# Experts in tiles of 256 rows instead of 384, with three of eight weight chunks split in advance and read back as halves

## What is computed

```python
h = h + attn(layernorm(h))                       # softmax(q k^T + causal) v, 16 heads
# mixture of experts, x = layernorm(h), E=4, K=2, D=256, F=1024
top_p, top_i = top_k(softmax(x @ router_w + router_b), 2);  top_p /= sum(top_p)
out = sum_e gate[t, e] * ((silu(x @ w1[e]) * (x @ w3[e])) @ w2[e])
h = h + out
h = h + recurrence(layernorm(h))
h = h + quantised_ffn(layernorm(h))
```

## Time and profile before

| | |
|---|---|
| median of three runs | 1753.79 us (1750.0 to 1754.49) |
| the profiled execution's own time | 1756.17 us |
| its span | 1754.3 us, 30236 instructions |
| granted TensorE clock, mean | 0.92 of full speed |
| TensorE busy | 1476.7 us, 84% of the span |
| VectorE, ScalarE, GpSimd busy | 1223.8, 989.0, 927.4 us |
| attention | about 86 to 830 us |
| expert stage, first to last matmul | 848.6 to 1394.8 us |
| recurrence and quantised layer | 1404 us to the end |
| DMA in all | 150.38 MB, mean 86 GB/s |

### The profile page before, as it was taken

How to read it: one execution, slowest core, us unless ns; L and a number is a source line. 1 busy time by engine, 2 the same in 40 slices (tenths; PEclk the granted TensorE clock), 3 DMA queues, 4 the chain that set the end, 5 groups by cost and what they waited for, 6 DMA issues and landing times. The chain is left out here.

```text
span 1754.3 us, 30236 instructions
## 1 busy us (share of the span) xinstructions
PE 1476.7 (84%) x10725; PEld 1374.2 (78%) x10725; DVE 1223.8 (70%) x2590; ACT 989.0 (56%) x2138; POOL 927.4 (53%) x750
## 2 busy tenths in 40 slices
PE   5389999999999999995699999999988746789039
PEld 4279888888888888885699999999987745788039
DVE  7548677777777777774256666666588489459896
ACT  4547675757575757572455555555543444459552
POOL 4468475858585858572567677776755623000000
PEclk8679999999999999997799999999999968899569
DMA  7490000000000100001665555555544321003313
GB/s 241 147 309 19 19 19 28 28 28 28 28 28 25 31 25 14 25 13 34 193 167 142 138 146 136 148 135 149 140 122 107 66 89 43 11 0 133 110 51 113
DMA packets 86126, 150.38 MB, mean 86 GB/s; under 512 B 7992, under 2 KB 63608, under 8 KB 85720
## 3 DMA queue, kind: packets, MB, share of 16 engines
q1 hardware_dynamic: 75464, 134.62, 24.7%
q0 software_dynamic: 10512, 13.83, 4.6%
HBM read 111.88 MB, written 49.91 MB: 92 GB/s over the span
## 5 line engine op out<-in xcount | busy, mean ns | idle before, releaser
L1589 POOL TENSOR_TENSOR expert_w_low<-expert_raw,expert_w_high 128x768 fp32r<-128x768 f32 x152 | 288.5, 1948 | 172.1 <-ACT expert_w_high L1414 167.0
L855 ACT ACTIVATE expert_raw<-psum,neg_max 120x376 f32<-120x376 f32 (+2 forms) x384 | 176.9, 486 | 106.0 <-DVE neg_max L1041 103.8
L1561 DVE TENSOR_TENSOR expert_act_low<-expert_act,expert_act_high 128x384 fp32r<-128x384 f32 x152 | 140.0, 921 | 79.6 <-ACT expert_act_high L1452 79.0
L1452 ACT ACTIVATE expert_act_high<-expert_act 128x384 fp32r<-128x384 f32 x152 | 79.8, 525 | 204.1 <-DVE expert_act L1556 202.7
L967 POOL TENSOR_TENSOR qk_low<-rotated,qk_high 128x376 fp32r<-128x376 f32 x128 | 127.0, 992 | 95.2 <-ACT qk_high L848 95.2
L1373 PE MATMUL psum<-slots_high,expert_w_high 128*128 128x384 f32 x608 | 161.0, 346 | 16.7 <-DVE expert_act L1556 15.4
L1064 DVE TENSOR_TENSOR pt_low<-psum,pt_high 128x752 fp32r<-128x752 f32 x128 | 120.4, 941 | 69.9 <-ACT pt_high L864 69.5
L1373 PE MATMUL psum<-slots_low,expert_w_high 128*128 128x384 f32 x608 | 157.0, 339 | 0.0
L1373 PE MATMUL psum<-slots_high,expert_w_low 128*128 128x384 f32 x608 | 156.7, 338 | 0.0
L1384 PE MATMUL psum<-expert_w_high,expert_act_high 128*128 128x256 f32 x456 | 134.5, 295 | 11.6 <-ACT slot_out L1434 9.9
L997 POOL TENSOR_TENSOR rotated<-rotated,expert_raw 128x376 f32<-128x376 f32 x128 | 127.7, 998 | 14.5 <-POOL expert_raw L993 0.5
(11 more groups left out here) (305 smaller groups left out, 4380.6 us busy)
## 6 DMA issues: line engine op xcount, KB each, us to landing
expert_raw<-in_experts SPq DMA_DIRECT2D x152, 384.0 KB, 3.1
x_slots<-in_c_slots SPq DMA_DIRECT2D x4, 3168.0 KB, 27.8
slot_rows<-x_slots SPq DMA_DIRECT2D x19, 396.0 KB, 4.5
up_spill<-held SPq DMA_DIRECT2D x5, 1128.0 KB, 5.0
held<-up_spill SPq DMA_DIRECT2D x5, 1128.0 KB, 5.7
attn_x<-tok_xt SPq DMA_DIRECT2D x6, 752.0 KB, 4.0
x_parts<-attn_x SPq DMA_DIRECT2D x6, 752.0 KB, 4.6
patch<-in_patches SPq DMA_DIRECT2D x8, 376.0 KB, 6.8
```

Source lines behind the costliest of these rows:

```text
L855: last = act.activation(probs[0:ni, h % 2, at:at + P * it + ni], score_bank(h % 2, it), ACT.Exp, bias=neg_max[0:ni, h % 2, it:it + 1], acc ...
L1561: dve.tensor_tensor(act_hl[1][:, g % 2, :], act_f[:, g % 2, :], act_hl[0][:, g % 2, :].bitcast(F32), ALU.subtract).then_inc(low_made, 1)
L1589: pool.tensor_tensor(w[1][:, g % RING, :], raw[:, g % RAW, :], w[0][:, g % RING, :].bitcast(F32), ALU.subtract).then_inc(w_low, 1)
```

## The change

There are two edits that belong together.

**Tiles of 256 rows.** TILE_SLOTS goes from 384 to 256. EXPERT_TILES becomes 27 (before 19), BLOCKS 2 (before 3); rows of all tiles go from 7296 to 6912, chunks from 152 to 216, and weight loads with them. All ACT, DVE and PE work that goes by TILE_SLOTS gets 256 columns; the split of a weight chunk keeps its 768.

**Chunks 2, 4 and 6 are split once** (KEPT_SPLIT). There are 4 experts times 3 such chunks, 12 jobs, two at the beginning of each of batches 1 to 6. A job loads the chunk over `whole` (columns of `expert_raw` that held the raw and swapped projections), ACT copies it into `parts[0]` (`pt_high`), POOL makes `parts[1]` (`pt_low`), and SP stores both to `split_w` in DRAM. The second job of a batch uses the same buffers, and step (b, 0) of ScalarE waits until all of it is stored. In the expert stage these chunks come as two halves, 768 KB, straight into `both` (`expert_w`), after `down` of the chunk eight before; ACT and POOL no longer split them.

Two small tables (`past`, `place`) move into `resid`.

```diff
-TILE_SLOTS = 384
+TILE_SLOTS = 256
...
+KEPT_SPLIT = (2, 4, 6)
+KEPT_RAW = tuple(f for f in range(CHUNKS) if f not in KEPT_SPLIT)
+SPLIT_JOBS = [(e, k) for e in range(EXPERTS) for k in range(len(KEPT_SPLIT))]
+SPLIT_BATCHES = range(1, 1 + len(SPLIT_JOBS) // 2)
...
@@ attention
+        whole = shared[:, 0:CHUNK_COLS]
+        parts = [x[:].rearrange("p u k n -> p (u k n)")[:, 0:CHUNK_COLS] for x in pt]
...
+                def load_whole(j):
+                    e, k = SPLIT_JOBS[j]
+                    sp.dma_start(whole, a["experts"][e, KEPT_SPLIT[k], :, :]).then_inc(whole_in, 16)
+
+                def store_parts(j):
+                    e, k = SPLIT_JOBS[j]
+                    sp.wait_ge(parts_low, j + 1)
+                    for part in range(2):
+                        sp.dma_start(split_w[e, k, :, part, :], parts[part].bitcast(F32)).then_inc(parts_stored, 16)
+
                 for b in range(BATCH + 1):
+                    if b in SPLIT_BATCHES:
+                        sp.wait_ge(rot_made, 16 * b + 2 * LEAD + CR_ROT)
+                        load_whole(2 * b - 2)
+                        store_parts(2 * b - 2)
+                        load_whole(2 * b - 1)
+                        store_parts(2 * b - 1)
                     if b:
                         sp.wait_ge(out_kept, T * b)
...
+                def split_part(j):
+                    act.wait_ge(whole_in, 16 * (j + 1))
+                    act.wait_ge(parts_stored, 32 * j)
+                    act.activation(parts[0], whole, ACT.Copy).then_inc(parts_high, 1)
+
                 def begin(b):
                     for at, t in enumerate(VALUE_ORDER):
+                        if at == 1 and b in SPLIT_BATCHES:
+                            split_part(2 * b - 2)
+                            split_part(2 * b - 1)
...
+                    if c == 0 and b in SPLIT_BATCHES:
+                        act.wait_ge(parts_low, 2 * b)
+                        act.wait_ge(parts_stored, 64 * b)
                     turned_high(b, 2 * c)
...
+                def split_part(j):
+                    pool.wait_ge(parts_high, j + 1)
+                    pool.tensor_tensor(parts[1], whole, parts[0].bitcast(F32), ALU.subtract).then_inc(parts_low, 1)
...
+                        if n == 2 * LEAD - 1 and b in SPLIT_BATCHES:
+                            split_part(2 * b - 2)
+                            split_part(2 * b - 1)
...
@@ expert_tiles
                         g = CHUNKS * i + f
-                        if g >= RAW:
-                            sp.wait_ge(w_low, g - RAW + 1)
...
+                        if f in KEPT_SPLIT:
+                            if i:
+                                sp.wait_ge(down_made, g - RING + 1)
+                            k = KEPT_SPLIT.index(f)
+                            sp.dma_start(both[:, f, :, :].bitcast(F32), split_w[bass.ds(e, 1), k, :, :, :]
+                                         .rearrange("e p h c -> p (e h) c")).then_inc(split_in[k], 16)
...
-                    if g + AHEAD < last_chunk:
+                    if g + AHEAD < last_chunk and (g + AHEAD) % CHUNKS in KEPT_RAW:
                         split_high(act, g + AHEAD)
...
-                    if g + AHEAD < last_chunk:
+                    if g + AHEAD < last_chunk and (g + AHEAD) % CHUNKS in KEPT_RAW:
                         split_low(g + AHEAD)
```

More of the change, by code:

```diff
@@ L432 @@
 RAW_CHUNKS, EARLY_CHUNKS, AHEAD_ROWS = 4, 2, 4
+KEPT_SPLIT = (2, 4, 6)
+KEPT_RAW = tuple(f for f in range(CHUNKS) if f not in KEPT_SPLIT)
+SPLIT_JOBS = [(e, k) for e in range(EXPERTS) for k in range(len(KEPT_SPLIT))]
+SPLIT_BATCHES = range(1, 1 + len(SPLIT_JOBS) // 2)
 SHARED_COLS = 5 * TOK + 2 * (3 * P + TOK)
 def attention(nc, psum, h0_rows, x_dram, weights, a, consts, ident, x_slots, h_rows, onehot, where, shared, raw_w, w_in,
-              scattered, tables, made):
+              split_w, scattered, tables, made):
     ctx, sb, sem = scopes(nc, made)
@@ L484, in attention @@
         ends = sb("tile_ends", [P, EXPERTS])
-        past = sb("past", [P, EXPERT_TILES, EXPERTS])
+        past = resid[:, 0, 0:EXPERT_TILES * EXPERTS].rearrange("p (t e) -> p t e", e=EXPERTS)
         owner = sb("owner", [P, EXPERT_TILES])
         start_of = sb("start_of", [P, EXPERT_TILES])
-        place = sb("place", [P, 2, EXPERT_TILES])
+        place = resid[:, 1, 0:2 * EXPERT_TILES].rearrange("p (k t) -> p k t", k=2)
         slots_cleared = sem("slots_cleared")
+        whole_in, parts_high, parts_low, parts_stored = (sem(f"split_w_{n}") for n in ("in", "high", "low", "stored"))
         (summed, std_made, rstd_made, x_made, x_turned, xt_kept, logits_made, odds_read, shifted, odds_made,
@@ L1254, in _, with expert_tiles @@
                 dve.wait_ge(table_made, 1)
-def expert_tiles(nc, psum, a, x_slots, h_rows, onehot, where, raw, w_in, added, ident, vec, first, turn, feed, up_gate, down,
+def expert_tiles(nc, psum, a, x_slots, h_rows, onehot, where, raw, w_in, split_w, added, ident, vec, first, turn, feed, up_gate, down,
                  spent, made):
@@ L1264, in expert_tiles @@
         xt = [sb(f"slots_{part}", [P, 2, 2, TILE_SLOTS], F32R) for part in ("high", "low")]
-        w = [sb(f"expert_w_{part}", [P, RING, CHUNK_COLS], F32R) for part in ("high", "low")]
+        both = sb("expert_w", [P, RING, 2, CHUNK_COLS], F32R)
+        w = [both[:, :, part, :] for part in range(2)]
         silu = sb("silu", [P, 2, TILE_SLOTS])
@@ L1302, in group_dst @@
             return dst if len(dst.shape) == 3 else dst.rearrange("p (k n) -> p k n", k=GROUP)
+        split_in = [sem(f"expert_split_in{k}") for k in range(len(KEPT_SPLIT))]
+        raw_of = lambda g: len(KEPT_RAW) * (g // CHUNKS) + KEPT_RAW.index(g % CHUNKS)
         three = ((0, 0), (0, 1), (1, 0))
@@ L1435, in keep_out @@
                                    scale=gate[:, i % 2, 1:2]).then_inc(y_kept, 1)
-                split_high(act, 0)
-                split_high(act, 1)
-                keep_high(0, 0)
-                keep_high(0, 1)
-                split_high(act, 2)
-                split_high(act, 3)
+                for g in range(AHEAD):
+                    if g == EARLY_CHUNKS:
+                        keep_high(0, 0)
+                        keep_high(0, 1)
+                    if g in KEPT_RAW:
+                        split_high(act, g)
                 for g in range(last_chunk):
@@ L2311, in audio_tower @@
             attention(nc, psum, h0_rows, x_dram, weights, a, consts, ident, x_slots, h_rows, onehot, where, shared,
[L2312 removed]
+                      raw_w, w_in, split_w, scattered, tables, front_sems)
         held = ctx.enter_context(nc.sbuf_tensor("held", [P, UPS * QCHUNKS * TOK], F32))
@@ L2323, in audio_tower @@
             expert_sems, late_sems = [], []
-            expert_tiles(nc, psum, a, x_slots, h_rows, onehot, where, raw_w, w_in, added, ident, vec, first, turn, feed, up_gate,
+            expert_tiles(nc, psum, a, x_slots, h_rows, onehot, where, raw_w, w_in, split_w, added, ident, vec, first, turn, feed, up_gate,
                          down, front_sems, expert_sems)
```

33 lines of the change are left out of this document (22 added, 11 removed).

## The result

The changed kernel takes 1789.94 us (median of 4 runs, 1787.22 to 1793.17) beside 1754.14 us for the kernel before on the same chip: ratio 1.0204, interval 1.0183 to 1.0225, so 2.0% longer, as forecast (1791.8 us, range 1744 to 1822). The profiled execution's span is 1785.4 us, 31.1 more than before, where the medians are 35.8 apart: the profiled execution of the changed kernel is the shortest of its four, that of the kernel before lies 2 us above its median.

A forecast was written before the change was run, and what follows sets the result against it. TensorE was taken as the bound, busy 84% and filling plain tiles. Expert stage +17.3, table doubling +2.1 and attention +18.6 made +38.0 us on 1756.2, 1794.2, less 2.4 for the median: 1791.8 us, range 1744 to 1822.

The forecast's parts named there:

- TensorE's own work: Expert stage matmuls: chunk 2.14 us, tile 17.5 us, 473 us against 494, 21 us less if nobody waits.
- Rival C: Expert stage: 256-column up matmuls still start every 0.174 us, tile 22.9 us, total about 1900 us; chance 0.03.
- A plain tile: Expert tile without extra work: scaled result 0.7 us late for down of chunk 0, so 18.2 us.
- A quantised tile: Expert tile that measures, rounds or turns quantised weights: 21.8 us, 3.6 us above a plain one.
- Measure: Quantised tile: VectorE's small tensor_scalar waits for GpSimd's split, the product of chunk 4 is late, 1.1 us lost.
- Low part of f = 6: Quantised tile, rounding: GpSimd's split of f = 5 delays VectorE's low part of chunk 6, 0.6 us lost.
- Product of f = 7: Quantised tile: VectorE rounds for 1.7 us, the product of chunk 7 ends late, 1.0 us lost.
- Scaled result: Quantised tile: kept group and split of f = 7 push the last tile's result to 17.6 against 16.3, 1.3 us lost.
- Table doubling: Expert chunks under table doubling: VectorE, ScalarE and GpSimd form a ring; +21.3 us against +19 before, +2.1 us more.
- Attention: Start of each batch: two jobs form one chain delaying ScalarE's probabilities, 3.1 us in 6 batches, +18.6 us.
- A: Other engines still keep up with TensorE, expert stage 21 us less, attention +6, total 1739 us; chance 0.17.
- B: Expert stage: DMA full, loads land late behind down(6), +27 us at 1 us a tile, total 1819 us; chance 0.13.

The follow-up runs named there:

- the fastest kernel: 256-row kernel with VectorE's work moved and spread (1712.64 us), changed so ScalarE and VectorE scale the finished tile's result first at f = 1: 1700.44 us, ratio 0.9697.
- the best kernel with the old height: 384 rows, three chunks pre-split, second job in the o buffers (1722.44 us), with measuring and table steps moved: 1710.76 us, ratio 0.9751.

## Why the prediction was right, and where it was off

The mechanism held: TensorE's shorter work was outweighed by waits for products, low parts and scaled results that operations of fixed size make late, and attention paid for the chain of jobs.

- **TensorE's own work.** Nearly right. A clean chunk is 2.16 us (0.120 a matmul) where I had 2.14, and the tile without waits is 17.7 us, not 17.5, which takes 5 of the 21 us. Rival C is out.
- **A plain tile.** Low: 0.7 us of waits forecast, all of it for the scaled result; 18.72 - 17.7 = 1.0 measured, half of it for the low part of f = 6. The cause was named (three splits and the add at f = 3, 4, 5); I took an add at 1.2 us, and it is 1.56. Moving that add took the whole 1.0 us away.
- **A quantised tile.** Measure: 1.1 us forecast, 1.11 measured in the tile from 1008 us. Low part of f = 6: 0.6 and 0.72. Product of f = 7: 1.0 and 0.64. Scaled result: 1.3 and 0.86. From start to start of the matmuls the four cost about 4.3 us, against 4.0 forecast. The mean over the 13 is 22.13 against 21.8. My terms, 1.1, 0.6, 1.0, 0.15, 1.3 and 0.3, add to 4.45 and not to 4.3, which is 2 us over 13 tiles. The run with the scatter moved shows the low part's wait to be a collision; the run with VectorE's work moved shows of the others that place decides and not amount.
- **Table doubling.** +21.3 us over plain tiles forecast, 75.5 - 3 x 18.7 = 19.4 measured; only 2 us off. The 33.6 us that it started from held two stretches at half clock, which I had not looked for.
- **Attention.** The term that was mis-sized: 18.6 us forecast, 10.8 measured, 1.3 to 3.2 in each of five batches, 12.2 in those together; the stretch behind them scatters by 5 us from kernel to kernel. The first job's load was taken at 3.1 us and was about 3.0, but stores and second load took 4.7 us and not 5.0, and the last stores 3.4 and not 4.0. My steps as written also end at 275.95 + 3.1 + 2.8 + 5.0 + 2.8 + 4.0 = 293.65, not at 294.05, which is 2.7 us a batch and about 16 in six; and all batches got the same. The run with the second job in o confirms the place: removing that chain's tail gives all of it back.
- **Sum.** The expert stage came to 23.7 us where I had 19.4, attention to 10.8 where I had 18.6, and the end of the stage gave 2.4 us that I had left at nothing. In the traces that is 31.1 us against my 38.0, 7 us off although the errors partly cancel. The medians are 35.8 apart, since the changed kernel's profiled execution is 2.7 us under its median and that of the kernel before 2.0 above. That the total came within 2 us of the forecast is luck on both counts.
- **Rivals.** A needed the product late by less than 2.0 us; in quantised tiles it was not, until VectorE's extra work was moved. Its time, 1739 us, is passed by the same work in another order (1727.23 us). B, the DMA, is refuted in the fastest kernel too: it moves 255 GB/s at a share of 0.84 without a wait. By the working that gave 262 GB/s as the most it could carry, the share there would be 0.97, so that working was not sound.
- What I had not seen is how much of the change was a gain covered by a loss: I priced it as one step. Separated, the pre-splitting is worth 17 us at the old height, even with its price in attention, and the height alone costs 95.

## What to carry to other kernels

Halving or trimming a tile shortens the time between two needs of TensorE, while operations whose size is set by something else (a weight split, a scatter) stay as long; look first for the longest of these on the neighbouring engines and what it blocks. When an operation in the trace is several times its usual length, find what ran on the engine that shares its memory port and move one of the two, before cutting any work. And when a change has two parts, price and run each alone: here one was worth keeping and the other paid only after several changes of order, 10 us over the best kernel with the old height.

## What was not expected of the hardware

- One GpSimd scatter of 1.56 us ahead of a split cost 23 us of the expert stage, over 27 tiles, because VectorE then met the split from its start. A low part took 0.43 us alone, 1.0 in the usual collision, and 4.22 against two splits in a row: it came in only behind the second, so a port that is locked for one instruction was not handed over between two.
- TensorE's clock: one wait of 2.4 us for VectorE, at the end of a tile of the run with the height alone, was followed by a window at 0.50. The Trainium skill (TensorE: Matmul & The Clock Gate, Part 1: The HAM clock gate) describes such a fall to half rate after idling. The windows above agree on the two levels, but TensorE had not been idle throughout before the fall: it was busy for 1.22 and 0.71 of 2.16 us. In a plain tile the fall cost about 0.6 us, against 2.5 for the wait itself.
- A load of both halves of a chunk, 768 KB in one piece, landed in 4.3 us by the median, sooner than the 384 KB loads beside it (5.0 us, and 3.1 in the kernel before), and but for ScalarE's 2.0 us no engine waited for either.
